# Key gathers of a relational graph attention kernel: six slots and a lead of five batches instead of three and two, and four gathers under way in both layers

## The reference, cut to what matters

```
def rgat_conv(x, W, q, k, b, src, dst, etype, heads, out_ch, n_nodes):
    xr = jnp.einsum('nd,rdf->rnf', x, W)          # the projections, one for each relation
    oi = xr[etype, dst]; oj = xr[etype, src]
    qi = oi @ q                                    # the "query" of an edge's target
    kj = oj @ k                                    # the "key" of an edge's source
    alpha = jax.nn.leaky_relu(qi + kj, NEG_SLOPE)
    m = jax.ops.segment_max(alpha, dst, num_segments=n_nodes)
    e = jnp.exp(alpha - m[dst])
    z = jax.ops.segment_sum(e, dst, num_segments=n_nodes)
    a = e / (z[dst] + EPS)
    msg = (a[:, :, None] * oj.reshape(-1, heads, out_ch)).reshape(-1, heads * out_ch)
    return jax.ops.segment_sum(msg, dst, num_segments=n_nodes) + b

h = relu(layernorm(x)); x = x + gcn(h)             # layer 0
h = relu(layernorm(x)); h = elu(rgat_conv(h, ..1)) # layer 1
x = x + rgat_conv(h, ..2)                          # layer 2
```

## Time and profile before

| what | us |
|---|---|
| median of 3 runs (1609.24, 1615.69, 6044.12) | 1615.69 |
| profiled execution, its own time | 1607.11 |
| its span, first to last instruction | 1605.3 |
| PE busy / POOL busy / DVE busy | 1453.7 / 1000.9 / 901.0 |
| layer 1: first key gather, first score, last projection stage work of PE | 469.04, 500.82, 778.19 |
| layer 2: first key gather, first score, last projection stage work of PE | 1062.74, 1097.10, 1363.19 |

### The profile page before, as it was taken

The page is one execution under the profiler, slowest core; times in us unless marked ns, Lnnn a source line. Parts: engine busy times, 40 slices in busy tenths (PEclk is TensorE's granted clock), DMA queues, the critical chain, the costliest instruction groups (busy, mean ns, idle before and its releaser), DMA issues.

```text
span 1605.3 us, 24837 instructions
## 1 busy us (share of the span) xinstructions
PE 1453.7 (91%) x6446; PEld 878.0 (55%) x6450; DVE 901.0 (56%) x2002; ACT 274.0 (17%) x709; POOL 1000.9 (62%) x1112
## 2 busy tenths in 40 slices
PE   4988999999978999999699999769996999899996
PEld 2545555555566555666455555455553655455553
DVE  8677722334455888888688878406324445223333
ACT  2545300000011333323000124410110011000000
POOL 1599277666537777882477777336656662777673
PEclk9988999999987999899799999858997999899998
DMA  8300498899831131111588888701231111889898
GB/s 319 118 20 21 125 315 305 291 316 312 270 102 23 51 110 47 40 37 41 169 303 278 285 262 257 241 3 32 59 111 31 40 43 50 286 298 308 281 303 269
DMA packets 86811, 271.80 MB, mean 169 GB/s; under 512 B 32156, under 2 KB 32531, under 8 KB 86743
## 3 DMA queue, kind: packets, MB, share of 16 engines
q0 software_dynamic: 51072, 199.44, 39.3%
q1 hardware_dynamic: 34807, 65.62, 11.4%
q10 hardware_dynamic: 864, 5.90, 1.0%
HBM read 239.28 MB, written 31.62 MB: 169 GB/s over the span
## 4 chain that ended last, share of the span: by engine, by line
PE 61%; DMA 14%; POOL 10%; issue 7%; DVE 5%; ACT 1%; DVEq 1%; SPq 0%; POOLq 0%; ACTq 0%; PEldq 0%
PE ps L1293 12%; PE ps L1320 12%; PE ps L1359 12%; DMA ring<-keys,idxr 8%; POOL ring L519 8%; PE ps L1361 6%; PE ps L1362 6%; PE ps L1190 5%; DMA ring<-rows,idxr 3%; PE ps L1111 1%; PE ps L1236 1%; PE ps L1153 1%; PE ps L1254 1%; DVE zw L1020 1%; DVE hn L1017 1%
## 5 line engine op out<-in xcount | busy, mean ns | idle before, releaser
L1320 PE MATMUL ps<-wreg,hT 128*128 128x384 f32 x1440 | 486.7, 501 | 7.3 <-PEq L1313 6.6
L519 POOL DMA_INDIRECT ring<-keys,idxr x312 | 319.2, 1023 | 189.1 <-DMA ring<-keys,idxr 73.6
L488 POOL DMA_INDIRECT ring<-rows,idxr x304 | 303.7, 999 | 168.8 <-PEq L1348 60.9
L1320 PEld LDWEIGHTS ps<-wreg,hT 128*128 128x128 f32 x1440 | 280.6, 196 | 202.2 <-issue 23.5
L1359 PE MATMUL ps<-ring,zw 128*128 x664 | 224.0, 495 | 15.6 <-DVE zw L1088 15.0
L1293 PE MATMUL ps<-ring,zw 128*128 x664 | 221.3, 495 | 9.6 <-DVE zw L909 9.6
L488 POOL DMA_INDIRECT ring<-rows,idx x152 | 144.7, 952 | 97.1 <-PE ps L1293 66.0
L1359 PEld LDWEIGHTS ps<-ring,zw 128*128 128x128 f32 x664 | 124.7, 191 | 108.7 <-issue 34.2
L1086 DVE TENSOR_TENSOR ring<-ring,al x166 | 159.2, 959 | 39.4 <-SPq L406 30.7
L1293 PEld LDWEIGHTS ps<-ring,zw 128*128 128x128 f32 x664 | 127.5, 193 | 98.1 <-issue 15.3
L1091 DVE TENSOR_SCALAR zw<-iota_f,tl,al 128x128 f32<-128x128 f32 x166 | 60.8, 368 | 154.7 <-PE ps L1362 129.7
(11 more groups left out here) (189 smaller groups left out, 1314.0 us busy)
## 6 DMA issues: line engine op xcount, KB each, us to landing
wreg<-in_L_gnn_W SPq DMA_DIRECT2D x11, 2304.0 KB, 9.8
rows<-stage SPq DMA_DIRECT2D x30, 386.0 KB, 2.8
rows<-stage SPq DMA_DIRECT2D x30, 384.5 KB, 2.9
stT<-targets_row ACTq DMA_DIRECT2D x6, 960.0 KB
ring<-keys,idxr POOLq DMA_INDIRECT x312, 2.5
ring<-rows,idxr POOLq DMA_INDIRECT x304, 4.5
rows<-stT SPq DMA_DIRECT2D x10, 384.0 KB, 2.9
xs<-in_x SPq DMA_DIRECT2D x3, 1152.0 KB, 13.4
```

The costliest lines, as they stand in the source:

```text
L488: nc.gpsimd.indirect_dma_start(ring[:, t % (2 * RING), 0:WIDTH[l]], None, rows[l], bass.IndirectOffsetOnAxis(idx[:, t:t + 1], 0)).then_inc ...
L519: nc.gpsimd.indirect_dma_start(kb[:, n % KSEMS, t % KB, 0:4], None, keys[l], bass.IndirectOffsetOnAxis(idxr[:, t:t + 1], 0)).then_inc(k_in ...
L1320: last = mm(ps[:, 2 * (nt % 2) + h, 0:HALF], hT[:, k, nt * P:(nt + 1) * P], wreg[:, r % 2, k, h * HALF:(h + 1) * HALF], start=(k == 0), st ...
```

## The change

The number of key slots goes from 3 to 6; a new constant AHEAD = 5 takes the place of the lead of two batches; the number of gathers under way in layer 2 goes from 2 to 4, the same as layer 1 has already.

```diff
-KSEMS = 3
-KFLIGHT = {1: 4, 2: 2}
+KSEMS = 6
+AHEAD = 5
+KFLIGHT = {1: 4, 2: 4}
...
                 pool.wait_ge(s_keys, 16 * R * l)
-                ask_keys(0)
-                ask_keys(1)
+                for n in range(AHEAD):
+                    ask_keys(n)
                 pool.wait_ge(qs_ready, l)
                 for n in range(KSURE):
                     score(n, n % KSEMS, n + 1)
-                    if n + 2 < KSURE:
-                        ask_keys(n + 2)
+                    if n + AHEAD < KSURE:
+                        ask_keys(n + AHEAD)
```

## The result

The changed kernel takes 1672.59 us (median of 4 runs, 1671.01 to 1680.63) against 1616.05 before (median of 4 runs). The ratio is 1.0374, with a 95% interval of 1.0323 to 1.0426; it is that of the means of the fast runs, without the one of 6044.12 us. Its profiled execution took 1672.28 us with a span of 1670.5, 65.2 more than before. The forecast was 1677 and +67.5 on the profiled execution.

What follows compares the result with a forecast made beforehand. PE held 61% of the chain of waits, DMA 14%, POOL 10%; DVE set the end of layer 1's score stage. Layer 1 +44 and layer 2 +23.5 gave +67.5 us on 1607.11: 1674.6, stated as 1677, range 1652 to 1700.

Steps and rivals of the forecast that it cites:

- Layer 1, later beginning: Layer 1 scores: 36 more gathers at 1.25 us put score 0 and DVE's first pair 45.0 us later, uncovered.
- Layer 1, pace: Layer 1: batches stay 18.5 us apart, DVE saves only 1 us, ACT waits stay; layer 1 +44, bounds +25 and +47.
- Layer 2, later scores and four under way: Layer 2: score 6 behind 132 gathers, not 96, at 1.25 us; 179.6 us after the first; +23.5, bounds +15 and +57.
- Layer 2, after transpose 1, the clock: PE's 72 instructions behind a stop run slower, but such stops cost nothing new: taken at 0, bound +3.
- More slots: Slots in free memory and two more semaphores; extra POOL waits are on things long landed: 0.
- A: POOL: under 0.84 us a gather, layer 2's transpose 1 loses its 13.3 us wait; 1594 at best; chance 1%.
- B: Layer 2: the queue is slow, so four under way bring nothing; +44 + 57 = +101 us, 1708; chance 5%.
- C: Layer 1's delay partly made good by DVE and faster gathers: +25, with +15 in layer 2 +40, 1647; chance 7%.

Runs made afterwards that it cites:

- the first experiment: Gathers under way in layer 2 raised from 2 to 4, lead of two and three slots kept, against the kernel before: 1592.83 us, ratio 0.9901.

## Why the prediction was right, point by point

*The whole: right, and nearer than the working deserves.* The sum was +44 for layer 1, +23.5 for layer 2 and nothing elsewhere; measured were +46.4, +19.3 and -0.5. Part of the small difference between +67.5 and +65.2 is luck: 2.4 us too little and 4.2 too much nearly cancel, and before's own layer 1 differs by 3.5 us between two executions that should be alike.

*Layer 1, later beginning: right.* Predicted score 0 later by 45.0 us, measured 45.3 (548.02 - 470.90 = 77.1 behind the first gather instead of 31.8); PE predicted to stand from 518 to 548, stood from 522.5 to 552.1, with PE's projections beginning 3.6 later. A lead of three costs a third of it, and without the lead it is gone.

*Layer 1, pace: right in the mechanism, 2.4 us too small in size.* Scores 0 to 8 are 18.3 us apart (18.5 before). DVE made up none of the delay: its last maximum comes 46.5 us later behind the first key gather, its first pair 45.3. Predicted +44, measured +46.4 against before and +43.0 against the kernel with more slots alone. The term that I held fixed, the waits for ACT's masks, is the one that scatters: 9.0 us in the changed kernel, 4.5 before, 14.2 in one that begins like before.

*Layer 2, later scores and four under way: right.* Predicted 179.6 us from the first gather to score 6, measured 178.9; transpose 1 at 182.1 instead of the predicted 183. PE stood 26.1 us at transpose 0, as the prediction had it (1185 to 1212 in before's times). The experiments part it: 133.0 with four under way and a lead of two, 205.1 with two under way and a lead of five. The page "DMA: Bandwidth & Descriptors" of the Trainium skill, section "Anatomy of one DMA", says that the fixed time of a transfer is mostly the wait for its completion. The trace agrees: 67.5 us of landing waits became 5.7 by having more under way. The same section says that many descriptors can be emitted before their cost shows. Of that the runs show nothing: a gather kept POOL busy for 0.94 us, and the 36 gathers delayed score 0 of layer 1 by 45.3 us, 1.26 each.

*Layer 2, after transpose 1, the clock: the term that was mis-sized.* I took 0, with a bound of +3, and it measured -3.5, on the other side. The work behind transpose 1 took 137.6 us instead of 141.2, which with a transpose 1 that came 0.7 us earlier than forecast made layer 2 +19.3 instead of +23.5. The stop right before that transpose became shorter, 6.1 us instead of 13.3, and the next 72 instructions took 25.16 instead of 26.10: 0.9 us. The rest comes from two later places. From transpose 5 to 6 before took 20.65 us and the changed kernel 16.82; from transpose 2 to 3 it is the other way, 24.06 and 25.30. At the first of them before's execution had a lower granted clock, in the row of 1310 to 1320 us (length of the stretch, busy times of PE, PEld, DVE, ACT and POOL, then PEclk, DMA share, GB/s); the second row is the same work in the changed kernel:

```profile
1310.00:1320.00 10.00, 10.00 (x27) 5.69 (x26) 1.68 (x6) 0.98 (x2) 6.46 (x12) 0.84 0.04 1
```

```profile
1378.00:1388.00 10.00, 10.00 (x32) 5.89 (x31) 3.88 (x14) 1.47 (x3) 0.00 (x0) 1.00 0.10 39
```

This is no scatter of one execution: the kernel with more slots has 19.84 and 24.06 us at the same two places. Right ahead of the lower clock the 24 short matmuls behind transpose 5 (L1233) took 3.1 us in before, and 0.9 in the changed kernel. What made them slow, and whether the lower clock follows from it, stays open.

*More slots: right,* 0.9992.

*The rivals.* A (gathers so cheap that nothing is lost) is refuted by the steps of 1.25 us; its gain, PE's wait in layer 2, exists and comes when the lead is left at two. Its point of decision was set too high: by its own reading layer 2 can give back only PE's 13.3 us, however early score 6 comes, so that the 36 gathers of layer 1 would be made good at 13.3 / 36 = 0.37 us for a gather and not at 0.84. B (four under way bring nothing) is refuted by the first experiment. C (part of the delay of layer 1 made good) hardly was: +46.4 against before, +43.0 against the kernel with more slots, for a beginning 45.3 later.

## What to carry to other kernels

In this kernel a prefetch distance was free only as long as the engine that issues would otherwise have waited. Count what the distance costs on the issuing engine, and compare it with the date at which the first result can be used: here two batches, 24 gathers, fit in before the queries are ready, each further one delays the first score by 15 us, and with only one the landing of each batch shows. Then ask who waits for that result: layer 1 paid nearly all of the delay, layer 2 paid 6.5 of 15.3 us for the third batch, since PE came to its transpose later. How far ahead one asks and how many are under way at a time are separate knobs; four under way at a lead of two gain 1%, and only that half should be kept.

## What the runs showed of the hardware that I had not expected

Behind most stops TensorE's next work is slower, so that the stop costs more than its length. With a wait of 13.15 us before transpose 1 (the kernel with more slots), the next 72 instructions take 26.07 us, after a wait of 5.56 (a lead of three) 24.56, without one 23.39:

```profile
1224.28 0.66 PE L1339 MATMUL ps<-ident,zw 128*128 128x128 f32 x2 [13.15 <-DVE mx L991]
1224.74 26.07 PE L1321 MATMUL ps<-wreg,hT 128*128 128x384 f32 x72
```

```profile
1229.22 0.66 PE L1339 MATMUL ps<-ident,zw 128*128 128x128 f32 x2 [5.56 <-DVE mx L991]
1229.68 24.56 PE L1321 MATMUL ps<-wreg,hT 128*128 128x384 f32 x72
```

But what is lost behind a stop does not grow steadily with its length. The same number of instructions takes 24.79 us after a wait of 12.44 and 24.93 after one of 48.60 (the lead alone), 25.16 after 6.13 and 26.16 after 26.12 (the changed kernel), and after 3.68 us (a lead of one) as little as without a stop:

```profile
1232.91 0.41 PE L1339 MATMUL ps<-ident,zw 128*128 128x128 f32 x2 [3.68 <-DVE mx L991]
1233.15 23.39 PE L1321 MATMUL ps<-wreg,hT 128*128 128x384 f32 x72
```

What decides between these is not shown.

The granted clock in the stretch with the stop is a mixture of the levels of 1.2 and 2.4 GHz: 0.57 in 1210 to 1230 us of before, where PE has no work until 1222.02, and still 0.60 in its second half, in which PE works; in 1230 to 1240 it is 1.00. It is 1.00 in 1210 to 1230 us of the kernel with four under way alone (the rows are of before, before and that kernel):

```profile
1210.00:1230.00 20.00, 7.98 (x17) 4.66 (x18) 8.62 (x31) 0.49 (x1) 12.49 (x16) 0.57 0.10 22
```

```profile
1220.00:1230.00 10.00, 7.98 (x17) 4.66 (x18) 8.35 (x30) 0.49 (x1) 6.03 (x7) 0.60 0.04 3
```

```profile
1210.00:1230.00 20.00, 20.00 (x65) 11.90 (x64) 8.54 (x31) 2.45 (x5) 15.24 (x18) 1.00 0.19 50
```
